# A transformer layer on one core: the rows of maxima of each attention group issued by GpSimd's queue instead of SyncE's

## What is computed

```python
def bitnet_linear(x, weight, scale_param):
    s = jnp.maximum(jnp.mean(jnp.abs(weight), axis=1), 1e-08)
    binary_w = jnp.sign(weight / s[:, None])
    y = jnp.einsum('bsi,oi->bso', x, binary_w)
    y = y * (s * scale_param)[None, None, :]
    return jnp.nan_to_num(y, nan=0.0, posinf=1000000.0, neginf=-1000000.0)
...
x = x + _L0_attn_ref(_layernorm(x, axis=-1), ...)
x = x + _L0_ffn_ref(_layernorm(x, axis=-1), ...)
# attention: softmax over keys of q k / 4, times v
# feed-forward: silu(x W1) * (x W3), times W2, with W = base + mean|w - base| * sign(w - base)
```

## Time and profile before

| | |
|---|---|
| median of 3 runs | 988.2 us (987.72 to 992.29) |
| profiled execution | 992.83 us, of which 991.0 us are the span |
| attention stage in the span | about 57 to 468 us |
| feed-forward stage | about 475 us to the end |

### The profile page before, as it was taken

How to read it: one execution, slowest core, us unless ns; L and a number is a source line. 1 busy time by engine, 2 the same in 40 slices (tenths; PEclk the granted TensorE clock), 3 DMA queues, 4 the chain that set the end, 5 groups by cost and what they waited for, 6 DMA issues and landing times.

```text
span 991.0 us, 14763 instructions
## 1 busy us (share of the span) xinstructions
PE 949.2 (96%) x5030; PEld 619.1 (62%) x5030; DVE 713.4 (72%) x948; ACT 548.2 (55%) x1076; POOL 303.8 (31%) x312
## 2 busy tenths in 40 slices
PE   7799999999999998988999999999999999999998
PEld 6444443444344433333777888888888888888886
DVE  6687898889878897876876588655886558854443
ACT  5458889989999998976654322323223232232221
POOL 4754658365636431527100111111101110101110
PEclk9879999999999999999999999999999999999999
DMA  6534655465546566632652002310023100220001
GB/s 183 133 111 125 185 170 177 152 208 177 157 135 187 155 198 198 183 110 87 226 164 85 1 0 86 125 51 1 1 86 129 46 0 0 85 86 0 0 0 42
DMA packets 75668, 105.14 MB, mean 106 GB/s; under 512 B 9944, under 2 KB 33496, under 8 KB 75608
## 3 DMA queue, kind: packets, MB, share of 16 engines
q1 hardware_dynamic: 74776, 103.26, 33.5%
q0 software_dynamic: 448, 0.46, 0.3%
q10 hardware_dynamic: 384, 0.66, 0.2%
HBM read 74.59 MB, written 28.05 MB: 104 GB/s over the span
## 4 chain that ended last, share of the span: by engine, by line
PE 77%; DVE 7%; DMA 4%; ACT 4%; issue 3%; POOL 2%; SPq 2%; DVEq 0%; POOLq 0%; ACTq 0%
PE psum L1755 15%; PE psum L1756 15%; PE psum L1757 15%; PE psum L1654 8%; PE psum L1644 8%; PE psum L1628 6%; PE psum L1535 3%; PE psum L1536 2%; DMA q_slot<-shift 2%; DVE nmx L1261 2%; ACT probs L1076 1%; PE psum L1667 1%; PE psum L1668 1%; SPq L404 1%; DVE stage L1376 1%
## 5 line engine op out<-in xcount | busy, mean ns | idle before, releaser
L1261 DVE TENSOR_REDUCE nmx<-psum 128x2 f32<-128x1024 f32 x256 | 305.2, 1221 | 64.2 <-PE psum L1628 62.1
L1076 ACT ACTIVATE probs<-psum 128x512 f32<-128x512 f32 x512 | 270.7, 602 | 45.4 <-PE psum L1644 43.6
L933 POOL CAST dh<-w2T 128x512 fp32r<-128x512 f32 (+1 forms) x56 | 49.2, 878 | 418.7 <-PE psum L1757 402.0
L1755 PE MATMUL psum<-fxh,wh 128*128 128x512 f32 x448 | 175.4, 392 | 0.0
L1756 PE MATMUL psum<-fxl,wh 128*128 128x512 f32 x448 | 174.5, 390 | 0.0
L1757 PE MATMUL psum<-fxh,wl 128*128 128x512 f32 x448 | 174.4, 389 | 0.0
L1644 PE MATMUL psum<-q_slot,k_slot 50*128 50x512 f32 x512 | 151.3, 473 | 16.3 <-ACT probs L1076 6.6
L1644 PEld LDWEIGHTS psum<-q_slot,k_slot 50*128 50x128 f32 x512 | 64.8, 187 | 134.1 <-ACT probs L1076 64.3
L1654 PE MATMUL psum<-probs,v_slot 128*32 128x512 f32 x1024 | 139.8, 619 | 0.0
L1132 ACT ACTIVATE hh<-gate 128x512 fp32r<-128x512 f32 x56 | 35.5, 633 | 167.8 <-DVE gate L1445 167.8
L1127 ACT ACTIVATE gate<-psum 128x512 f32<-128x512 f32 x56 | 33.5, 599 | 169.5 <-PE psum L1757 169.5
(11 more groups left out here) (146 smaller groups left out, 1331.6 us busy)
## 6 DMA issues: line engine op xcount, KB each, us to landing
stage<-in_L_ffn_mean_w_dram SPq DMA_DIRECT2D x60, 256.0 KB, 3.7
q_slot<-q_stack SPq DMA_DIRECT2D x180, 64.0 KB, 2.3
stage<-in_L_ffn_w_dram SPq DMA_DIRECT2D x42, 256.0 KB, 3.8
weighted_values<-u_sb SPq DMA_DIRECT2D x32, 256.0 KB, 2.4
k_slot<-k_stack SPq DMA_DIRECT2D x60, 96.0 KB, 2.4
an<-weighted_values SPq DMA_DIRECT2D x16, 256.0 KB
al<-reciprocals SPq DMA_DIRECT2D x16, 256.0 KB
x<-_attn_hidden_states_dram SPq DMA_DIRECT2D x8, 512.0 KB, 4.3
```

Of the source, the lines that this page charges most:

```text
L933: nc.gpsimd.tensor_copy(dh[parity][:], w2T[:, bass.ds(src, 1), :].rearrange("p o c -> p (o c)")).then_inc(dh_ok, 1)
L1076: nc.scalar.activation(probs[kt][:, j, :], BANK[ring_bank(("score", g, kt, j))], ACT.Exp, scale=HEAD_DIM ** -0.5).then_inc(exp_ok, 1)
L1261: v.tensor_reduce(column, pair, AX.X, ALU.max, negate=True).then_inc(s_max, 1)
L1755: mm(o, lhs_hi, rhs_hi, start=first, stop=False)
```

## The change

`load_shift` leaves SyncE's program: there it was the first step of each group's program, and the first one stood before the weight tiles. It is now a step of GpSimd's: once before `guard_item(0, 5)`, and then at the head of slice kt = 2 of each group for the next group. What it sends, and the semaphores, are the same.

```diff
--- before.py
+++ after.py
@@ -538,19 +538,11 @@
         group_stored(2)
         load_group(sp, 2, 2, slot_in[2])
 
-        def load_shift(g, s):
-            for part, ready in enumerate((sh_hi, sh_lo)):
-                r = ROWS + part
-                sp.wait_ge(ready, g + 1)
-                sp.dma_start(q_slot[s][r:P:HALF].bitcast(FP32).rearrange("h j (t c) -> h (j t) c", c=P),
-                             shift[s % 2][:, part, :].bitcast(FP32)).then_inc(shift_in[s], 16)
-
         def store_values(g, s):
             sp.wait_ge(u_ok, g + 1)
             sp.dma_start(u_dram.rearrange("b k r c t -> (b k r c) t")[bass.ds(P * g, P)], u_sb[s % 2][:]
                          ).then_inc(u_out[s % 2], 16)
 
-        load_shift(0, 0)
         load_difference(0, 0)
         load_difference(0, 1)
 
@@ -603,8 +595,6 @@
 
             b, at = divmod(4 * g, SLICES)
             s = g % 4
-            if g < LAST_G:
-                load_shift(g + 1, (s + 1) % 4)
             if g + 3 < GROUPS:
                 positive(sp, t_mm, 16 * g)
                 group_stored(g + 3)
@@ -844,6 +834,17 @@
         fill_values(1)
         norm_tokens(1, 2)
         norm_tokens(1, 3)
+
+        def load_shift(g):
+
+            s = g % 4
+            for part, ready in enumerate((sh_hi, sh_lo)):
+                r = ROWS + part
+                pool.wait_ge(ready, g + 1)
+                nc.gpsimd.dma_start(q_slot[s][r:P:HALF].bitcast(FP32).rearrange("h j (t c) -> h (j t) c", c=P),
+                                    shift[s % 2][:, part, :].bitcast(FP32)).then_inc(shift_in[s], 16)
+
+        load_shift(0)
         guard_item(0, 5)
 
         def difference(e, k):
@@ -884,6 +885,8 @@
         def pool_slice(g, kt):
 
             b, at = g // KV_HEADS, 4 * (g % KV_HEADS) + kt
+            if kt == 2 and g < LAST_G:
+                load_shift(g + 1)
             if 4 * g + kt == 3:
                 split_item(0, 5)
             if kt == 3 and g + 2 < GROUPS:
```

## The result

The changed kernel took 1035.3 us in the median of 4 runs (1032.51 to 1036.8), beside 988.6 us (also 4 runs) for the kernel before: a ratio of 1.0476 with an interval of 1.0436 to 1.0517, so 47 us slower. The forecast was 995 us. The sign was right; the size was not: the forecast was 7.1 us slower, so it was too small by a factor of nearly seven.

What follows compares the result with a forecast made beforehand. TensorE, busy 96% of the span, was taken as the bound, so only its stops counted. Terms 4.3 + 3.9 + 0.9 + 1.9 + 2.0 - 5.9 = +7.1 us on 988.2 gave 995 us, range 986 to 1003.

Steps and rivals of the forecast that it cites:

- The stops before groups 0, 7 and 15: GpSimd reaches its pairs late in its own order, so TensorE stops 4.3, 3.9 and 1.9 us before these groups.
- L = 3.0: Assumed landing time in us of a shift on GpSimd's queue, one value for all groups, range 2.0 to 4.9.
- the term for the bulk: SyncE's bulk loads, in flight when the shift is sent, delay it: 0 to 4.4 us given back, taken as +2 us.
- Groups 11 and 19: no stop: The shift lands just before TensorE wants it at these groups: cover 0.2 us, no stop.
- group 25: cover 1.2 us: Shortest time between shift and group with GpSimd free: landing 374.26, wanted 375.48, so no stop.
- The clock: After the stop before group 7 TensorE's clock falls, costing 0.9 us.
- The relief of -5.9 us: Shift off SyncE's queue, loads move ahead: 4.4 us of TensorE stops, 0.9 of clock, 0.6 of key waits saved.
- Hidden: Rival: GpSimd's queue lands as fast as SyncE's, L = 2.0, nothing lost to the bulk; 990.3 us, not slower; chance 0.25.
- Loads win: Rival: SyncE's relief counts as the chain counts it, 15.4 us against 8.0 of stops; 980.8 us, faster; chance 0.09.
- Slow software queue: Rival: shifts on GpSimd's queue take L = 4.0, stops also at groups 11 and 19; 1002.3 us; chance 0.19.
- VectorE holds the issue up: Rival: VectorE's maxima behind each shift delay GpSimd's descriptor writes, every pair 1.2 us later; 1000.9 us; chance 0.06.

Runs made afterwards that it cites:

- experiment 1: The changed kernel with SyncE's old wait put back, so its loads and bulk start only when the shift is ready; GpSimd still sends it: 1004.2 us, ratio 1.0188.
- 4: The changed kernel with SyncE's loads held until the shift is ready and GpSimd's pairs issued earlier for groups 0, 7 and 15: 995.9 us, ratio 1.0093.
- number 5: The changed kernel, SyncE's loads early as there, with GpSimd's pairs issued earlier for groups 0, 7 and 15: 1024.5 us, ratio 1.0331.
- number 9: The changed kernel, slot loads early as there, with SyncE's bulk held until the shift has landed; pairs not moved: 1007.8 us, ratio 1.0178.
- number 10: The changed kernel with SyncE's bulk held until the shift has landed and GpSimd's pairs moved forward for groups 0, 7 and 15: 994.6 us, ratio 1.007.
- number 7: The kernel before, shift still on SyncE, with the slot loads of group g+3 put ahead of the shift and the bulk behind: 982.9 us, ratio 0.9934.
- number 8: The kernel before with slot loads ahead of the shift, both on SyncE, and the bulk held until the shift has landed: 988.7 us, ratio 1.0016.
- 6: The changed kernel with slot loads early as there, but SyncE's bulk behind them held until the shift is ready: 1023.4 us, ratio 1.0359.

## Why the prediction was right in sign and wrong in size

**Right.** SyncE's 154.0 us at the shift went, its slot loads start with their group, and the added issues, 37.7 us, were hidden. The stops before groups 0, 7 and 15 are there with 4.25, 4.19 and 2.83 us (11.3 in all, against a forecast of 10.1). At 7 and 15 the terms are right too: by the chain those landings took 3.25 and 3.39 us, close to L = 3.0. At group 0 the right number is luck. The shift landed in 1.81 us, not 3.0, and GpSimd was later than forecast: it began its pair at 53.35, 1.6 us after TensorE wanted the shift (56.03 - 4.25 = 51.78), where 0.7 was forecast. The two errors cancel. Moving the pairs forward gave 8.3, 10.8 and 13.3 us in three pairs of runs (1 and 4, the change and 5, 9 and 10), which is this part with its clock. Single executions of one kernel lie up to 14 us apart (number 5), so these are rough.

**The step that failed** is the term for the bulk: "This is not earned in full if the bulk loads, now in flight when the shift is sent, delay it: between 0 us and the 4.4 us given back whole. I take the middle, +2 us". The mechanism was named, and its bound was wrong. It took the stops that the old order had left as the most that the new order could cause. But those 4.4 us were measured with the bulk held back by the very wait that the change removes; they bound nothing of what comes when the wait is gone. Measured: 21.7 us of stops in seven groups, and 31 us of the median, with the clock, when the wait is put back (experiment 1). With GpSimd's pairs moved forward in both, it is 30 us (numbers 5 and 10). A better bound was at hand. The earlier trace rows has the very same transfer in flight for 7.38 and 5.54 us on SyncE's queue, and the earlier trace rows has 7.9 us for a transfer in the crowded opening, and SyncE's bulk stands at every group's end. An estimate from rows: group 25 has 375.48 - 370.71 - 0.55 = 4.2 us from its second issue until it is wanted, a landing of 7.9 leaves 3.7 of stop, and a few such groups give the right order of size.

**The second fault is of the same kind**: one L for all groups. The change's own landings are 1.7 at least, 2.6 in the median and 9.7 at most. L = 3.0 was near the middle, and the middle is not what matters; where a group has 2 to 4 us of cover the tail decides. "Groups 11 and 19: no stop" and "group 25: cover 1.2 us" fell by it (6.47, 5.67 and 2.06 us).

**The clock** was costed once, at 0.9 us. In the attention stage it was some 19 us more than before. Ten stops instead of three are one reason: by windows of half a microsecond the clock was low behind nine of them (not behind the 1.09 us before group 4), for about 4 to 14 us each, and once more, for some 10 us, with no such stop before it. The other is the price of one fall. The 0.9 us counts eight matmuls; the 4 us of the earlier trace rows at 0.57 give 4.0 x (1 - 0.57) = 1.7 us for the same fall.

**The relief of -5.9 us** was mostly there to be had. The key waits and the stops before groups 5 and 28 went; the one before group 26, which the prediction had go, stayed at 2.99 us (3.28 before). Number 7 earned 5.8 us in the median (988.7 beside it, 982.9) by the early slot loads alone. The two profiles place 2.5 us of that between group 0 and group 31 (400.7 us before, 398.2 in number 7), as much as the stops by the shift fell (4.4 to 1.9); where the rest lies is open.

**The rivals.** *Hidden* and *Loads win* are out. *Slow software queue* put every landing at 4.0 us or more. The median was 2.6, and those that held TensorE took 1.8 to 9.7; it was right that many groups would stop, for the wrong reason, and its 1002.3 us was still too small. The queue by itself is as quick as SyncE's to about 0.1 us: 1.8 us in the median of number 9, against 1.7 for group 9 in number 8 (168.00 - 165.71, less the 0.56 until the second issue). The Trainium skill, "DMA: Bandwidth & Descriptors", section "Latency and other measured facts", has the first bytes of the two paths 0.4 us apart; of landings, which are what is measured here, the runs say 0.1. *VectorE holds the issue up* is out: over all 64 issues one took 0.557 us at least, 0.572 in the median and 0.730 at most, and VectorE took maxima beside them, as from 202.32 to 204.68 beside the pair at 203.71.

**What stays open.** Which of the bulk transfers does the most (item stores, tokens, tiles) was not tried one by one; neither was why the low clock lasts about 4 us after one stop and over 18 after another, nor what GpSimd as the sender costs by itself. Nor was a cure tried for the stops near group 26, 1.87 us in number 7.

## What to carry to other kernels

A queue's wait for something small can be what keeps large transfers from starting until the small one has gone. Before taking it away, list what stands behind it, and take the landing time in a crowd, the longest and not the median, against each group's cover. If a queue has idle time, move ahead of the urgent transfer only what has landed by the time it is sent, and leave the bulk behind it: that order beat the kernel before by 0.7% here (interval 0.3 to 1.0%), and the changed one by about 5%.

## What the runs showed of the hardware that was not expected

- The second of two DMAs of 8 KB landed in 1.7 to 1.8 us with little else in flight (SyncE's and GpSimd's queues), and in up to 9.7 (GpSimd's queue), 8.9 (SyncE's) and 7.7 us (ScalarE's) with stores, tokens and a weight tile in flight. Another queue was no protection.
- Small loads issued beside it slowed it as well: 5.11 us against 1.82 with the eight slot loads going out at that moment (numbers 6 and 1, group 0).
- A stop of TensorE of 2.66 us (number 9, group 7) was followed by more than 18 us at 1.2 GHz, one of 6.47 us in the change by 5.1 us. The first cost more after its end than during it: the group took 16.9 us, where number 10 had 12.4.
